# The fourth stage's routing moved into the attention ahead of it: a four-layer network in one kernel on Trainium2

## The reference

```python
xn = _layernorm(x, axis=-1)
# attention, single head, "upper": masked where the upper triangle's score is 0
scores = jnp.einsum('bqd,bkd->bqk', q, k) / jnp.sqrt(jnp.float32(d_k))
scores = jnp.triu(scores, k=0)
scores = jnp.where(scores == 0, MASK_NEG, scores)
s = softmax(scores) @ v
# feed-forward: 8 experts, each row goes through the one with the largest gate
xr = x @ wg_red.T                      # 128 -> 16
wg_unit = wg / jnp.maximum(jnp.linalg.norm(wg, axis=1, keepdims=True), EPS)
gates = jax.nn.softmax(xr @ wg_unit.T, axis=1)
indices_s, scores = jnp.argmax(gates, axis=1), jnp.max(gates, axis=1)
for e in range(E):                     # here x stands for xn
    mask = (indices_s == e).astype(x.dtype)[:, None]
    h = jax.nn.gelu(x @ w1[e] + b1[e], approximate=False)   # 128 -> 512
    out = out + mask * (h @ w2[e] + b2[e])                  # 512 -> 128
out = out * scores[:, None]
x = x + s * silu(out)
```

## Time and profile before

| | |
|---|---|
| median of three runs | 6226.08 us |
| the profiled execution | 6231.22 us, its span 6229.5 us |
| granted TensorE clock, mean | 0.969 |
| TensorE, VectorE, ScalarE, GpSimd busy | 91%, 70%, 62%, 47% of the span |
| fourth attention, first turn to last division | 5680 to 5895 us |
| fourth feed-forward, first instruction to end | 5899.7 to 6229.5 us, its tiles from 6058 us |

### The profile page before, as it was taken

One profiled execution on the slowest core, in us unless ns is written; L12 is line 12 of the kernel. 1 busy time (PEld: TensorE's weight loads), 2 busy tenths in 40 slices (PEclk: granted clock), 3 DMA queues, 4 the chain that ended last, 5 costly groups with the idle time before them and its releaser, 6 DMA issues. The chain is left out here.

```text
span 6229.5 us, 102190 instructions
## 1 busy us (share of the span) xinstructions
PE 5679.5 (91%) x33881; PEld 3007.7 (48%) x33881; DVE 4332.5 (70%) x9866; ACT 3859.4 (62%) x8225; POOL 2930.6 (47%) x2790
## 2 busy tenths in 40 slices
PE   8999999689997999999999899999999999987738
PEld 3444444422222666666666534444444444465528
DVE  4555554178885777777778678888888888786625
ACT  2444444156665777777777577777777777764416
POOL 1224325457766776666666433232332332243358
PEclk9999999799998999999999999999999999999969
DMA  2001001221101111111111100000000000023353
GB/s 46 15 15 40 24 17 44 77 61 31 41 24 33 43 31 32 31 32 42 43 42 44 40 21 12 19 11 12 19 11 12 19 12 12 8 84 107 104 184 100
DMA packets 345691, 248.86 MB, mean 40 GB/s; under 512 B 28224, under 2 KB 321090, under 8 KB 344914
## 3 DMA queue, kind: packets, MB, share of 16 engines
q1 hardware_dynamic: 325120, 202.06, 12.3%
q0 software_dynamic: 12544, 29.71, 1.3%
q10 hardware_dynamic: 7506, 10.56, 0.5%
HBM read 109.78 MB, written 90.71 MB: 32 GB/s over the span
## 5 line engine op out<-in xcount | busy, mean ns | idle before, releaser
L3839 PE MATMUL a_scores_ps<-a_kT,a_q_mixed 128*128 128x512 f32 x2048 | 1046.4, 593 | 3.2 <-ACT a_probs L3649 3.1
L3849 PE MATMUL a_acc_ps<-a_probsT,a_v_post 128*128 128x512 f32 x2048 | 1042.9, 592 | 0.4 <-DVE a_probsT L3742 0.4
L3649 ACT ACTIVATE a_probs<-a_scores_ps,a_neg_max 128x512 f32<-128x512 f32 x1024 | 702.9, 686 | 428.6 <-DVE a_neg_max L3732 419.2
L3732 DVE TENSOR_REDUCE a_neg_max<-a_scores_ps 128x1 f32<-128x512 f32 x1024 | 693.1, 677 | 202.0 <-PE a_scores_ps L3839 197.4
L3742 DVE STREAM_TRANSPOSE a_probsT<-a_probs 128x512 f32<-128x512 f32 x1024 | 715.1, 698 | 135.9 <-PE a_acc_ps L3849 110.7
L3654 ACT ACTIVATE a_probs<-a_probs,a_inv_sum 128x512 f32<-128x512 f32 x1024 | 727.6, 711 | 0.8 <-DVE a_inv_sum L3737 0.8
L3020 DVE TENSOR_REDUCE a_neg_max<-a_pair_ps 128x2 f32<-128x1024 f32 (+3 forms) x512 | 417.6, 823 | 357.7 <-PE a_pair_ps L3116 351.2
L2825 ACT ACTIVATE a_probsT<-a_pair_ps 128x1024 f32<-128x1024 f32 (+3 forms) x512 | 359.4, 704 | 485.4 <-PE a_pair_ps L3129 466.2
L3849 PEld LDWEIGHTS a_acc_ps<-a_probsT,a_v_post 128*128 128x128 f32 x2048 | 389.0, 190 | 490.9 <-issue 488.8
L3839 PEld LDWEIGHTS a_scores_ps<-a_kT,a_q_mixed 128*128 128x128 f32 x2048 | 384.4, 190 | 475.9 <-issue 437.7
L3595 POOL TENSOR_TENSOR a_q_mixed<-a_qT,a_pre 128x512 f32<-128x512 f32 x248 | 250.2, 1041 | 758.7 <-PE a_scores_ps L3839 758.7
(11 more groups left out here) (420 smaller groups left out, 11879.8 us busy)
## 6 DMA issues: line engine op xcount, KB each, us to landing
f_v_even<-f_v_odd SPq DMA_DIRECT2D x224, 130.0 KB
attention_out<-a_s_out SPq DMA_DIRECT2D x64, 256.0 KB, 2.3
f_x<-x_after SPq DMA_DIRECT2D x64, 256.0 KB, 5.3
a_v<-a_v_rows SPq DMA_DIRECT2D x256, 64.0 KB
sorted_rows_x<-a_fill SPq DMA_DIRECT2D x18, 772.0 KB
f_x_tiles<-sorted_rows_x SPq DMA_DIRECT2D x18, 772.0 KB
routes_y_rows<-a_zeros SPq DMA_DIRECT2D x32, 256.0 KB
a_parts<-routes_y_rows SPq DMA_DIRECT2D x32, 256.0 KB, 3.6
```

Of the source, the lines that this page charges most:

```text
L3649: act.activation(probs[:, n % NPR, :], scores_ps[n % NS][:], ACT.Exp, bias=neg_max[:, n % NS:n % NS + 1], scale=1.0, accum_out=row_sum[:, ...
L3732: dve.tensor_reduce(neg_max[:, n % NS:n % NS + 1], scores_ps[n % NS][:], AX.X, ALU.max, negate=True).then_inc(max_ready, 1)
L3839: pe.matmul(scores_ps[n % NS][:], q_mixed[:, g % 2, i].rearrange("f a q -> f (a q)"), kT[:, par, :], start=True, stop=True).then_inc(score ...
L3849: pe.matmul(acc_ps[par][:], v_post[:, g, i, :], probsT[:, g % NT, i, :], start=(p == 0), stop=(p == U - 1)).then_inc(products_done, 1)
```

## The change

The separate router stage goes. Its pieces are put into the attention's bodies, on the x that is there already:

- `rows` holds all 16 batches in SBUF with room for everything that is scattered; GpSimd normalises and divides straight into it. The attention's output is no longer stored, nor x loaded again.
- TensorE gets `reduce_rows` at k = 2 and `route_rows` at k = 3, ScalarE `keep_reduced` at k = 3, VectorE `keep_logits` at k = 0. All share the one PSUM bank `x_ps` with the turned rows.
- The sorting is done for groups of batches (0 to 4, 5 to 8, 9 to 11, 12 and 13, 14 and 15), by 20 small VectorE operations per group (`route`), two count matmuls (`count`) and a `carry` of rows per expert. Each expert has a segment of its own in the table, so that a place doesn't hang on later rows.
- GpSimd scatters a group's rows two a step after its places are known (`scatter_step`).
- The fill of the whole table becomes one pad of 128 rows behind each expert's last row. The experts' weights are loaded during the attention.
- The tile stage, `routed_experts_phase`, starts with the tiles. SyncE loads each of the 72 tiles with a transfer of its own, whose place it reads from `at_row`. Its ring of groups is 6 (4 before), the ring of picked weights 4 (3 before).

```diff
@@ the attention, SyncE
+            for b in range(4, batches):
+                sp.wait_ge(xn_ready, NC * (b - 3))
+                load_x(b)
+            sp.wait_ge(fill_ready, 2)
+            for e in range(E):
+                at = sp.value_load(fill_row[0:1, e:e + 1], min_val=0, max_val=E * SEGMENT - P)
+                sp.dma_start(routed_rows.x[bass.ds(at, P), :], fill[:]).then_inc(filled, 16)
+            sp.wait_ge(filled, 16 * E)
@@ the attention, GpSimd
+                for g, (first, last) in enumerate(GROUPS):
+                    begin = NC * (last + 1) if last <= LAST else NC * last + 3
+                    for at in range(NC * (last - first)):
+                        b = first + at // NC
+                        when = begin + at // 2
+                        if last > LAST:
+                            when = max(begin, NC * (b + 2) + (at % NC) // 2)
+                        if when == NC * n + k:
+                            scatter(b, at % NC)
@@ the attention, ScalarE, k = 3
+                    if k == 2 and group_ending(n) is not None:
+                        exp_diff(group_ending(n))
                     if k == 3 and exists(n + 1):
+                        keep_reduced(j.plus(1), n + 1)
                         keep_v(j.plus(1), n + 1)
@@ the attention, VectorE
+            def keep_logits(b):
+                dve.wait_ge(routed, b + 1)
+                dve.tensor_copy(logits[:, b * NC:(b + 1) * NC],
+                                x_ps[:, 0:NC * E].rearrange("p (c e) -> p c e", c=NC)).then_inc(logits_kept, 1)
...
+            def route_step(n, k):
+                g = group_ending(n)
+                if g is not None:
+                    for i in {0: range(0, 3), 1: range(3, 6), 2: (), 3: range(6, 9)}[k]:
+                        route(g, i)
+                g = group_ending(n - 1)
+                if g is not None:
+                    for i in {0: range(9, 12), 1: range(12, 16), 2: range(16, 20)}.get(k, ()):
+                        route(g, i)
@@ the attention, TensorE
+            def reduce_rows(j):
+                pe.wait_ge(xT_ready, j.of(1, 2))
+                pe.matmul(x_ps[0:GR, :], w_gate[:], xT[:], start=True, stop=True).then_inc(reduced, 1)
+
+            def route_rows(j):
+                pe.wait_ge(reduced_kept, j.of(1, 2))
+                for c in range(NC):
+                    last = pe.matmul(x_ps[:, c * E:(c + 1) * E], redT[:, c * P:(c + 1) * P], wg_unitT[:], start=True,
+                                     stop=True)
+                last.then_inc(routed, 1)
...
                     if k == 2 and exists(n + 1):
                         project(j, n, "k")
+                        reduce_rows(j)
                     if exists(n + o4):
                         products(j.plus(o4), n + o4, k4)
+                    if k == 0 and group_ending(n - 1) is not None and n - 1 != LAST:
+                        count(group_ending(n - 1), n)
                     if k == 3 and exists(n + 1):
                         project_v(j, n)
-
+                        route_rows(j)
@@ the tiles, SyncE
-            sp.wait_ge(scattered, 16 * N)
             for g in range(GROUPS):
-                load_group(g)
+                if g >= RING:
+                    sp.wait_ge(y_kept, g - RING + 1)
+                    sp.wait_ge(homes_ready, g - RING + 1)
+                for t in range(GROUP):
+                    i = g * GROUP + t
+                    at = sp.value_load(at_row[0:1, i:i + 1], min_val=0, max_val=E * routed_rows.SEGMENT - P)
+                    sp.dma_start(x_tiles[:, g % RING, t, :], routed_rows.x[bass.ds(at, P), :]
+                                 ).then_inc(tiles_loaded[g % RING], 16)
```

More of the change, by code:

```diff
@@ L1941, in bodies, with group_of, group_ending @@
                 body(Count(None, n), n)
+        def group_of(b):
+            return next(g for g, (first, last) in enumerate(GROUPS) if first <= b < last)
+        def group_ending(n):
+            for g, (first, last) in enumerate(GROUPS):
+                if last - 1 == n:
+                    return g
+            return None
         def turn_bank(what):
@@ new lines, in scatter @@
+            def scatter(b, c):
+                g = group_of(b)
+                if b == GROUPS[g][0] and c == 0:
+                    pool.wait_ge(route_chain, (g + 1) * PLACED)
+                    if g == 0:
+                        pool.wait_ge(tails_ready, 1)
+                if c == 0:
+                    pool.wait_ge(s_ready, NC * (b + 1))
+                row = b * NC + c
+                pool.indirect_dma_start(routed_rows.x, bass.IndirectOffsetOnAxis(ap=slot[:, row:row + 1], axis=0),
+                                        rows[:, b, c, :], None).then_inc(scattered, 16)
@@ L2017, in body @@
                         divide(j.plus(o4), n + o4, k4)
+                    scatter_step(n, k)
             bodies(pool, body)
+            for k in range(STEPS):
+                scatter_step(batches + 1, k)
+            pool.wait_ge(scattered, 16 * NC * batches)
         @block.scalar
         def _(act):
-            act.wait_ge(rows.x_loaded, 16)
+            act.wait_ge(x_loaded[0], 16)
             for dst, src in loads[1::2]:
@@ L2074, in body @@
                     if k == 1 and exists(n + 1):
-                        rows.keep_turned(act, x_ps, j.plus(1).number())
+                        keep_xT(j.plus(1))
                     if k == 2 and exists(n + 1):
@@ new lines, in _, with moments_of @@
+            dve.memset(fill[:, HOME:HOME + 1], float(routed_rows.NOWHERE)).then_inc(fill_ready, 1)
+            dve.wait_ge(gate_weights, 3)
+            chain(dve.tensor_scalar(wg_norm[:], wg_norm[:], 1e-4, None, ALU.max))
+            chain(dve.reciprocal(wg_norm[:], wg_norm[:]))
+            dve.tensor_scalar(wg_unit[:], wg[:], wg_norm[:], None, ALU.mult).then_inc(gate_weights, 1)
+            def moments_of(b):
+                dve.wait_ge(x_loaded[b], 16)
+                for c in range(NC):
+                    last = dve.bn_stats(stats[:, c, :], rows[:, b, c, X])
+                if b >= 1:
+                    dve.wait_ge(xn_ready, NC * b)
+                chain(last)
+                for c in range(NC):
+                    last = dve.bn_aggr(moments[:, c, :], stats[:, c, :])
+                chain(last)
+                dve.tensor_scalar(var_eps[:], moments[:, :, 1], EPS, None, ALU.add).then_inc(var_ready, 1)
```

570 lines of the change are left out of this document (253 added, 317 removed).

## The result

The changed kernel took 6194.32 us, the median of five runs (6192.15 to 6198.77), against 6227.55 us (6225.93 to 6233.77) for the kernel before on the same chip: a ratio of 0.9946, 95% interval 0.9932 to 0.9961, some 33 us faster. A second set of five gave 6192.90 and 0.9943 (0.9930 to 0.9957). The forecast was 6172.

What follows compares the result with a forecast made beforehand. It took a 163 us hole before the tiles, a ring of waits in the attention and GpSimd in the tile stage as bounds. Terms -142 + 58 + 26 + 4 = -54 us gave 6172 us from 6226.1; range 6120 to 6212.

Steps and rivals of the forecast that it cites:

- hole: Stretch from the attention's last reciprocal to the first tile's transposition: 163 us shrinks to 21, 142 us gained.
- ring: Cycle of waits between engines setting the attention's pace, 12.99 us a batch: grows 3.65 us, 58 us over 16 batches.
- five group steps: VectorE's twenty routing operations per group of batches, 17 of them ahead of a mask: 26 us added in all.
- start: Start of the attention: eleven loads come first, then a dozen small operations; 4 us added.
- tile stage: Stage of the experts' tiles, bound by GpSimd: stays at 2.06 us a tile, nothing counted.
- the first rival: TensorE's idle time in the attention swallows the logits, the added work hides: 54 us more gained, 6118 us; chance 0.12.
- So no gain from the clock: First tiles after the border: the granted clock stays at the lower level, 1.2 GHz, after a 20 us idle stretch.
- GpSimd as the bound by its scatters: Eight scatters in one attention batch make GpSimd the bound: 6184 us at 1.6 us each, 6222 at 2.2; chance 0.11.
- SyncE as the bound of the tiles: Tile stage: SyncE's 72 reads and issues set the pace beyond 2.06 us each, 6248 us at 3; chance 0.09.
- More scatters piled up behind the last division: Behind the attention: each scatter beyond eight costs 1.27 us, 43 would undo the forecast; part of the 0.06 chance.

Runs made afterwards that it cites:

- e11: Changed kernel with three useless matmuls at each of two places where TensorE waits, ahead of the projection to q and the logits; 6174.20 us (0.9912).
- e1: Changed kernel with ScalarE's copy of the reduction moved from k = 3 to the end of step k = 2; 6160.18 us (0.9886).
- e3: Changed kernel with the reduction ahead of the projection to k, its copy ahead of k's copy, the logits ahead of the projection to v; 6141.77 us (0.9857).
- e8: On e6, the two router matrices multiplied once at the start, so no reduction or copy of it per batch; 6110.37 us (0.9811).
- e6: On e3, most of VectorE's routing operations moved into its idle time and a group's scatters spread evenly over the steps; 6117.07 us (0.9820).
- e2: Changed kernel with two useless matmuls ahead of the projection to q, two ahead of the logits, and 40 unused semaphores; 6186.75 us (0.9934).
- e12: The changed kernel measured and profiled once more, nothing altered; 6192.90 us (0.9943).
- e4: Changed kernel with all 64 scatters issued behind GpSimd's last division, none in the attention's loop; 6265.47 us (1.0057).

## Why the prediction came out as it did

It was right in direction and in its mechanism, a closed hole against a longer ring; the range 6120 to 6212 held the time. The gain was 33 us for the 54 forecast. Against its sum, in the two profiled executions:

| term | predicted | measured |
|---|---|---|
| hole | -142 | -135.0 |
| ring, 16 batches | +58 | +58.6 (3.66 each) |
| five group steps | +26 | +22 |
| start | +4 | +2.9 |
| TensorE's clock in the attention | 0 | +19 |
| tile stage | 0 | -1.4 |
| stages ahead of the fourth attention | 0 | -5.6 |
| sum | -54 | -39 |

The attention, from its first instruction to the last reciprocal, grew from 226.3 to 329.2 us, by 102.8. In e11, with the clock at 1.00, it is 309.9, so 19 is the clock's; the group steps are what is left of the growth after ring, start and clock, and not measured by themselves.

**The ring** was read correctly from the earlier trace rows, 16.6 us a body for a measured 16.65. e1, e3 and e8 take its parts away one by one and land within 0.3 us of what it says: 14.73, 13.78, 13.07. That TensorE's idle time would hide the logits (the first rival) was wrong for this order of instructions. e8 shows that it is right for another order and a single matrix; the rival's 6118 was reached by moving instructions (e6, 6117), not by the change.

**The step that failed** is a line that I did not write. "So no gain from the clock" looked only at the tile stage; the attention's clock of 0.97 was taken as given, although the sum itself left TensorE 1.6 us more of waiting in each body (3.65 less 2.08 of work), and more beside the group steps. In the kernel before TensorE idles 2.8 us of 12.99 and keeps 2.4 GHz; in the changed one its waits come to some 4.3 of 16.65, 4.4 of 18.18 and 4 to 7 in the group bodies, single ones up to 3.2 us, and it falls to 1.2 GHz for stretches in 11 of 15 windows. e11 shows the cause: the same waits filled with useless matmuls, the clock at 1.00, 18.7 us less in the medians (6192.90 to 6174.20). Which waits bring a fall is not shown. The changed kernel's body of 18.47 us has 6.1 us of waiting and stays at 1.00; the kernel before bears waits of 1.63 us in every body; and in e2, where six windows still fall below 1.00, single waits of 0.98 or 0.99 us stand ahead of four of the six falls.

The Trainium skill, "TensorE: Matmul & The Clock Gate", section "Why this matters for your kernels", advises against idle gaps of more than about 3 us between bursts of matmuls. Four of the twelve falls here stand behind a wait of 3.0 to 3.2 us, in keeping with it, but eight behind 1.84 to 2.23 us, so the measurement goes further than the page.

**The hole** was 28.0 us for 21. The division and the scatters took 11.4 (10.7 predicted), since three of the scatters took 0.84 us more together beside VectorE's tables; that scatters beside a busy VectorE are not stretched, as the prediction has it, holds in the loop but not here. Four reads and issues at 1.1 us each made 4.1 up to the last issue (4.0); the landing took 2.6 (3.0). Landing of the scatters and border together were 9.85 instead of 3.4 (some 0.8 less in e12): I took them from a border behind a plain store, and behind scatters GpSimd's drain is 5.28 us, and only starts when the landing is over. The eight fills at 1.19 us and VectorE's tables (until 5998.3) were hidden, as said.

The Trainium skill, "DMA: Bandwidth & Descriptors", section "Latency and other measured facts", has 600 ns as a register read's floor. The trace does not agree, as far as the records of SyncE's instructions tell: of the 1.10 us from one issue to the next, the read's own record has a median of 0.27 us and at most 0.60, and the issue's a median of 0.34; register arithmetic and the steps between are the rest.

```profile
L1497 SPq TENSOR_LOAD <-routed_at_row x72: 6/268/599, 6013.6 to 6133.6; - x72
```

**The other rivals.** GpSimd as the bound by its scatters: refuted for this kernel by e4 (0.96 to 1.06 us each in the loop, some 1.27 from one to the next, and the body the same without them), but true once the body is 13.8 us, where eight of them cost 2.2 us (e3) and five nothing (e6). SyncE as the bound of the tiles: 1.10 us for a read and issue, under the 2.06 of a tile; refuted. More scatters piled up behind the last division: eight, as counted.

The 5.6 us ahead of the fourth attention are not the change's: that stage began at 5663.09 in the changed kernel, at 5668.66 before, and at 5668.10 in e12, the changed kernel profiled again (span 6195.0). Over all fourteen profiled executions, in none of which the code ahead was changed, it began between 5659.7 and 5669.8. So a single profile's place in the program is good to some 5 us either way, lengths are to be compared stage by stage, and the medians' 33 us is the better figure than the profiles' 39.

## What to carry to other kernels

When work is folded into a full pipeline, write down the ring of waits, and ask for each piece in whose idle time it could stand; here two matmul pieces and one copy cost 58 us on the ring, some 13 us in TensorE's waits (0.79 a body, e3), and about 1 us once one multiplied matrix made the reduction and its copy needless (e8). Count the waits that you add on TensorE as clock, too, and try useless matmuls there as a quick test of it. And price every engine again after each gain: scatters that were free at 16.65 us a body were the bound at 13.8.

## What was not expected of the hardware

- With no single wait above 3.2 us TensorE's granted clock fell to 0.76 to 0.92 of full over bodies of 18 to 21 us, in eight of twelve falls behind a wait of 1.84 to 2.23 us; other bodies with waits as long stayed at 1.00. At the lower level a pair of 512-column matmuls takes 1.89 to 2.04 us instead of 1.03 to 1.12.
- GpSimd's drain at the end of a block took 5.28 us with the last of 64 scatters just ahead, 1.57 with the last of 128 scatters 24 us back, 0.50 with none and 0.60 with one plain load long before. It can run beside the landing if another engine waits for that.
- A scatter took 0.96 us in most cases and up to 1.47 beside VectorE's operations on two SBUF inputs.
- 40 semaphores more to clear: 0.2 us (0.57 for 0.35).
- A register read and the issue of a load on SyncE: 1.10 us together, of which the read's own record is 0.27 and the issue's 0.34.
